# Cross-attention and linear attention on one core: interleaved last groups, four tile places, early sums, one ones-product per visit, maxima through DRAM

## The chip, the cores and the metric
One core of a Trainium2 chip runs the whole program. The metric is device time in microseconds (us) from start to end of one execution; the figure for a kernel is the median of its runs. Engines: TensorE (PE in the profile; its weight loads are PEld), VectorE (DVE), ScalarE (ACT), GpSimd (POOL) and SyncE (SP), whose queue issues all DMAs here. TensorE has a granted clock, given as a share of 2.4 GHz.

## The reference
Two layers on x (4 batches, 1024 rows, 512 features) and a context of the same size, all fp32.

```python
# layer 0: attention with 16 heads of 32, softmax, output projection, residual, layer norm
Q, K, V = x @ Wq.T + bq, ctx @ Wk.T + bk, ctx @ Wv.T + bv       # split in 16 heads
out = softmax(Q K^T / sqrt(32)) V @ Wo.T + bo
x = layernorm(out + x) * gamma0 + beta0
# layer 1: linear attention with phi = elu
KV = phi(ctx)^T ctx;  Z = 1 / (phi(x) . sum(phi(ctx)) + 1e-6)
x = layernorm(x + (phi(x) @ KV) * Z) * gamma1 + beta1
```

## The kernel before
**Units.** Heads go in groups of four (128 features); there are 16 groups (4 per batch). A unit is one group and one chunk of 256 queries: 64 units, of 16 ticks each, so 1024 ticks in which scores are computed. In tick k TensorE makes one 128x512 block of scores (`pass1`, L258), only for its row maxima (VectorE, L553). LEAD = 22 ticks later `pass2` (L282) makes the scores again the other way round (keys on partitions), with the row maximum subtracted inside the matmul: rows 96 to 103 of `q_stack` hold the negated maxima, those of `k_stack` a one-hot pattern. ScalarE takes the exponential into `p_ring` (L451, eight key tiles deep).

**Visits.** Every 8 ticks, from VISIT_AT = 35 on, TensorE visits four key tiles: `visit` multiplies the exponentials with V into `acc` (L300, 32 records) and sums them with a matrix of ones for the denominators (L308). For the sums GpSimd first adds the key tiles in pairs (`add_pair`, L760), in two halves of 512 columns. A visit takes two pair sums, 8 matmuls of 256 columns each, recorded as 16. `pair_sum` has two places, and a pair waits for the product of the pair two before it (`T["divided"]`). There are 128 visits. VectorE's `normalise` then inverts and scales `acc` into `outT` (20 units deep).

**Maxima.** VectorE's `split_max` reduces the maxima of a unit to `max_row` and splits them in two fp32r parts, `neg_max`. At tick 19 of the unit (PLACE) TensorE turns them with four matmuls (`place_max`, L267) in one of the score banks, and ScalarE copies the result into `q_stack` (L441).

**Chains.** The other work of TensorE is cut in chains, of which one piece is made in a tick (`beside`): K and V (projections of half a group's keys, 4 ticks), Q (a unit's queries, 2), O (output projection of one tile of 128 rows, 4), T (turning phi, 1), A (phi times KV, 4), S (one quarter of KV of a batch, 8 pieces), N (the sum of phi over the keys, 1), B (the bias of V through Wo, once, 4). A planner written in Python chooses the tick of each chain: no chain starts before `earliest`, the one with the first `deadline` goes first, and the table `after` holds what must be done before and how many ticks ago. All engines' queues are written out in the order of these ticks; SP's queue too, with waits in between. S needs `context_features`: two ScalarE operations and one on VectorE (L688) for each piece, and GpSimd's `add_features`.

**Tiles.** A tile of 128 rows goes O, y sum (L634), statistics, GpSimd's root (L773), ScalarE normalise (L473), GpSimd gamma and beta (L782, L784), ScalarE (L481, L483), phi (L656), T, A (L367), second norm, GpSimd gamma and beta (L789, L791), store. x, y and the feature arrays share the memory of the context (`ctx_nat`); there are two places (NX = 2), so tile i waits for the store of tile i - 2. A batch's tiles start when its last group is done, so those of the last batch run at the very end.

**The start.** FIRST = -44: K, V, Q chains of the first units stand before tick 0.

## Time and profile before

| what | value |
|---|---|
| runs | 1761.07, 1754.87, 1755.48 us; median 1755.48 |
| profiled execution | 1762.24 us, of which the span of the trace is 1760.9 |
| TensorE busy | 1646.2 us (93%), weight loads 1114.6 beside it |
| VectorE / ScalarE / GpSimd busy | 1070.9 / 880.9 / 951.3 us |
| granted clock, mean | 0.972 |
| DMA | 168 MB, mean 95 GB/s |

How to read it: a row of the stage view has a stretch (us from the span's start), its length, the busy time of PE, PEld, DVE, ACT and POOL with their numbers of instructions, the granted clock, the DMA engines' share and GB/s. A row by line has line, engine, operation, output<-input, shapes and count, then busy us, mean ns of one, and idle time just before them with what ended most of it. A row in order of time has start, duration, engine, line, operation, count, and in brackets the idle time before it. Durations of matmuls are modelled and overlap, so a stretch is better read from starts.

### The profile page before, as it was taken

How to read it: one execution, taken by the hardware profiler on the slowest of the kernel's cores; microseconds unless marked ns; L12 is line 12 of the kernel's file. 1: busy time of each engine (PE TensorE's matmuls, PEld its weight loads, DVE VectorE, ACT ScalarE, POOL GpSimd, SP SyncE). 2: the span in 40 equal slices, each digit the busy share in tenths (PEclk: the TensorE clock that was granted, in tenths of full speed). 3: DMA queues.
4: the chain of work that ended last, by engine and by line, in shares of the span. 5: the costliest groups of instructions: out<-in, count | busy, mean ns of one | idle time of the engine just before them, and what ended most of it. 6: DMA issues, size and time to landing. Idle time of an engine off the chain costs nothing.

```text
span 1760.9 us, 32310 instructions
## 1 busy us (share of the span) xinstructions
PE 1646.2 (93%) x12176; PEld 1114.6 (63%) x12176; DVE 1070.9 (61%) x2216; ACT 880.9 (50%) x1617; POOL 951.3 (54%) x923
## 2 busy tenths in 40 slices
PE   6999999999999999999999999999999999999754
PEld 4667776676766666567666657657676767665321
DVE  2665557656666666567566756666666666666232
ACT  0355547555554554654554554665545554575321
POOL 0244535455655664455665655555566555566644
PEclk8999999999999999999999999999999999999877
DMA  8524162233315244141523234322322423200001
GB/s 252 159 63 132 55 204 78 73 99 103 108 40 138 79 130 162 55 115 39 144 79 110 74 103 146 110 85 91 112 72 91 122 74 102 97 24 13 25 24 36
DMA packets 149291, 168.05 MB, mean 95 GB/s; under 512 B 12816, under 2 KB 111120, under 8 KB 149136
## 3 DMA queue, kind: packets, MB, share of 16 engines
q1 hardware_dynamic: 149136, 165.99, 31.8%
q8 instruction: 97, 1.59, 0.4%
q14 instruction: 58, 0.48, 0.1%
HBM read 124.00 MB, written 41.94 MB: 94 GB/s over the span
## 4 chain that ended last, share of the span: by engine, by line
PE 81%; DVE 6%; POOL 4%; DMA 4%; issue 3%; ACT 2%; SPq 1%; DVEq 0%; ACTq 0%; POOLq 0%
PE acc L300 13%; PE score L258 13%; PE scoreT L282 12%; PE misc L375 6%; PE misc L329 6%; PE misc L367 6%; PE acc L308 6%; PE misc L339 6%; PE misc L351 5%; PE misc L319 4%; DVE maxes L553 2%; POOL pair_sum L760 1%; PE score L267 1%; DMA res_out<-ctx_nat 1%; DMA ctx_nat<-ctx_in 1%
## 5 line engine op out<-in xcount | busy, mean ns | idle before, releaser
L760 POOL TENSOR_TENSOR pair_sum<-p_ring 128x512 f32<-128x512 f32 x512 | 654.5, 1299 | 636.0 <-PE acc L308 568.5
L553 DVE TENSOR_REDUCE maxes<-score 128x1 f32<-128x512 f32 x1024 | 679.1, 678 | 441.6 <-PE score L258 440.5
L451 ACT ACTIVATE p_ring<-scoreT 128x512 f32<-128x512 f32 x1024 | 595.6, 594 | 616.8 <-PE scoreT L282 603.5
L258 PE MATMUL score<-k_stack,q_stack 96*128 96x512 f32 x1024 | 615.6, 603 | 8.7 <-DVE maxes L553 7.5
L282 PEld LDWEIGHTS scoreT<-q_stack,k_stack 104*128 104x128 f32 x2048 | 378.7, 191 | 187.8 <-ACT p_ring L451 114.4
L282 PE MATMUL scoreT<-q_stack,k_stack 104*128 104x256 f32 x2048 | 428.0, 291 | 16.3 <-ACT p_ring L451 14.8
L258 PEld LDWEIGHTS score<-k_stack,q_stack 96*128 96x128 f32 x1024 | 194.3, 190 | 170.4 <-issue 139.2
L300 PE MATMUL acc<-p_ring,v_sb 128*32 128x256 f32 x4096 | 279.4, 392 | 0.0
L300 PEld LDWEIGHTS acc<-p_ring,v_sb 128*32 128x32 f32 x4096 | 155.5, 112 | 81.6 <-ACT p_ring L451 22.2
L308 PE MATMUL acc<-pair_sum,ones 128*32 128x256 f32 x2048 | 159.3, 383 | 7.7 <-POOL pair_sum L760 7.7
L319 PE MATMUL misc<-xT_sb,wq 128*128 128x256 f32 x512 | 134.3, 386 | 10.1 <-DVE k_low L615 5.8
L329 PE MATMUL misc<-ctxT_sb,wk 128*128 128x512 f32 x256 | 133.2, 606 | 7.7 <-DMA ctxT_sb<-ctxT_in 6.9
L367 PE MATMUL misc<-kv_sb,ctx_nat 128*128 128x512 f32 x256 | 135.3, 623 | 4.5 <-issue 2.3
L339 PE MATMUL misc<-wv,ctxT_sb 128*128 128x128 f32 x1024 | 134.1, 275 | 0.0
L375 PE MATMUL misc<-ctx_nat,fphi_sb 128*128 128x512 f32 x256 | 132.1, 597 | 0.0
L351 PE MATMUL misc<-wo,outT 128*128 128x512 f32 x256 | 129.5, 597 | 0.0
L339 PEld LDWEIGHTS misc<-wv,ctxT_sb 128*128 128x128 f32 x1024 | 125.8, 192 | 0.6 <-DVE k_low L615 0.3
L308 PEld LDWEIGHTS acc<-pair_sum,ones 128*32 128x32 f32 x2048 | 87.2, 112 | 46.5 <-POOL pair_sum L760 10.0
L319 PEld LDWEIGHTS misc<-xT_sb,wq 128*128 128x128 f32 x512 | 90.2, 193 | 18.9 <-DVE k_low L615 6.0
L773 POOL TENSOR_TENSOR rstd<-var_eps,minus_half 128x1 f32<-128x1 f32 x64 | 36.5, 571 | 92.8 <-DVE var_eps L648 92.6
L441 ACT ACTIVATE q_stack<-score 8x1024 fp32r<-8x1024 f32 x64 | 65.0, 1016 | 41.5 <-PE score L267 41.0
L688 DVE SCALAR_TENSOR_TENSOR fphi_sb<-f_sb,ctx_nat 128x128 f32<-128x128 f32 x128 | 70.1, 547 | 22.6 <-ACT f_sb L506 11.0
(66 smaller groups left out, 1221.8 us busy)
## 6 DMA issues: line engine op xcount, KB each, us to landing
xT_sb<-xT_in SPq DMA_DIRECT2D x64, 512.0 KB, 4.1
k_stack<-k_dram SPq DMA_DIRECT2D x96, 256.0 KB, 4.4
q_stack<-q_dram SPq DMA_DIRECT2D x192, 128.0 KB, 2.5
ctxT_sb<-ctxT_in SPq DMA_DIRECT2D x8, 1024.0 KB, 7.3
k_dram<-k_high SPq DMA_DIRECT2D x32, 256.0 KB, 2.0
k_dram<-k_low SPq DMA_DIRECT2D x32, 256.0 KB, 2.6
q_dram<-q_high SPq DMA_DIRECT2D x64, 128.0 KB, 1.7
q_dram<-q_low SPq DMA_DIRECT2D x64, 128.0 KB, 1.9
```

Of the source, the lines that this page charges most:

```text
L258: pe.matmul(score[use % 3][:], q_stack[0:SPLIT, unit % NQ, j, t * P:(t + 1) * P], k_stack[0:SPLIT, unit // NC % 2 * QUAD + j, h * HALF:(h ...
L282: mm = pe.matmul(scoreT[k % 2][:, (j % 2) * CH:(j % 2 + 1) * CH], k_stack[0:ROWS, unit // NC % 2 * QUAD + j, kt * P:(kt + 1) * P], q_stack ...
L300: mm = pe.matmul(acc[j * DK:(j + 1) * DK, 0:CH], v_sb[:, group % 2, kt, j * DK:(j + 1) * DK], p_ring[:, n % NP, j * CH:(j + 1) * CH], star ...
L308: mm = pe.matmul(acc[j * DK:(j + 1) * DK, CH:2 * CH], ones[:, 0:DK], pair_sum[:, pair % 2, j * CH:(j + 1) * CH], start=False, stop=part == ...
L319: mm = pe.matmul(bank_of("Q", unit)[:, 0:CH], wq[:, t, :], xT_sb[:, unit % 2, t, :], start=t == 0, stop=t == G - 1)
L329: mm = pe.matmul(bank_of("K", i)[:], wk[:, t, :], ctxT_sb[:, h, t, :], start=t == 0, stop=t == G - 1)
L339: mm = pe.matmul(bank_of("V", i)[:, t * P:(t + 1) * P], ctxT_sb[:, h, f, t * P:(t + 1) * P], wv[:, f, :], start=f == 0, stop=f == G - 1)
L367: mm = pe.matmul(bank_of("A", tile)[:], phiT_sb[:, d * P:(d + 1) * P], kv_sb[:, d, :], start=d == 0, stop=d == G - 1)
L375: pe.matmul(bank_of("S", i)[:], fphi_sb[:, piece % NPHI, :], ctx_nat[:, t, :], start=t == 0, stop=t == KT - 1).then_inc(T["kv_piece"], 1)
L451: act.activation(p_ring[:, n % NP, h * HALF:(h + 1) * HALF], scoreT[k % 2][:], ACT.Exp, scale=SCALE).then_inc(A["exped"], 1)
L553: dve.reduce_max(maxes[:, unit % 2, t, j, h:h + 1], score[bank_use[k] % 3][:], AX.X).then_inc(V["maxed"], 1)
L760: pool.tensor_tensor(pair_sum[:, pair % 2, cols], p_ring[:, (n - 1) % NP, cols], p_ring[:, n % NP, cols], ALU.add).then_inc(L["paired"], 1)
```

## The change
Five things at once.

1. **One ones-product per visit.** After the pair sums, GpSimd adds the two pair sums of a visit for columns 0 to 511 (`add_quad`, 128 times), VectorE those of columns 512 to 1023 (its own `add_quad`, two ticks before the visit), and the visit makes one product. The two places of `pair_sum` alternate so that the odd pair alone waits for a product and the even pair for the two quad sums.
2. **Maxima through DRAM.** `place_max` goes on both engines. `neg_max` is 128x32, VectorE turns it in blocks of 32 (`max_turned`), SP writes four blocks of 16 rows x 128 B to DRAM (`put_max`) and reads them back over the four heads into `q_stack` (`stack_max`). LEAD goes from 22 to 26, and VISIT_AT to LEAD + 13.
3. **The first linear sums come early.** S of batch 0 may start at tick 0 (before: 176), its context is loaded at tick -14, FIRST is -24, B moves to `outT` as its source, `wq` has two places.
4. **The last batch's last two head groups take turns**: their eight units are ordered (0,0) (0,1) (1,0) (0,2) (1,1) (0,3) (1,2) (1,3) as (group, chunk).
5. **Four places for the last batch's tiles**, for x and y each, in the memory of `ctxT_sb`, which is free by then; x is loaded when the last K and V projections are done.

```diff
-    LEAD = 22
-    PLACE = 19
-    VISIT_AT = 35
-    FIRST = -44
+    LEAD = 26
+    VISIT_AT = LEAD + 13
+    FIRST = -24
+    def place_of_pair(pair):
+        return (pair // 2 + pair % 2) % 2
+    order = [(b, b * G + g, chunk) for b in range(B) for g in range(G) for chunk in range(NC)]
+    order[-2 * NC:] = [(B - 1, GROUPS - 2 + g, chunk) for g, chunk in
+                       ((0, 0), (0, 1), (1, 0), (0, 2), (1, 1), (0, 3), (1, 2), (1, 3))]
+    def slot_of(tile):
+        return tile % NX if tile < TILES - KT else NX + tile % 4
+    def before(tile):
+        if tile < TILES - KT:
+            return tile - NX
+        return tile - 4 if tile >= TILES - KT + 4 else -1
...
             if kind == "N":
-                return UT * UB * i + 200
+                return UT * UB * i + 200 if i > 0 else FIRST
             if kind == "S":
-                return UT * UB * b + 176 + 8 * t
-            unit = UB * b + UB - NC + t // TPC
-            spaced = UT * UB * b + 242 + TILE_TICKS * t
-            return max(UT * unit + 50, spaced if b < B - 1 else 0)
+                return UT * UB * b + 176 + 8 * t if b > 0 else 0
+            spaced = UT * UB * b + LEAD + 220 + (TILE_TICKS if b < B - 2 else TILE_TICKS - 4) * t
+            return max(UT * unit_at[G * b + G - 1, t // TPC] + LEAD + 28, spaced if b < B - 1 else 0)
...
-                for s in range(VISIT // 2):
-                    pair = VISIT // 2 * v + s
-                    pe.wait_ge(L["paired"], 2 * (pair + 1))
-                    for j in range(QUAD):
+                pe.wait_ge(L["quad_low"], v + 1)
+                pe.wait_ge(V["quad_high"], v + 1)
+                for j in range(QUAD):
...
+            def add_quad(v):                                   # VectorE
+                first, second = (pair_sum[:, place_of_pair(2 * v + i), HALF:2 * HALF] for i in range(2))
+                dve.wait_ge(L["paired"], 4 * (v + 1))
+                dve.tensor_tensor(first, first, second, ALU.add).then_inc(V["quad_high"], 1)
...
+                elif h == 0 and pair >= 2:                     # GpSimd, add_pair
+                    pool.wait_ge(L["quad_low"], pair // 2)
+                    pool.wait_ge(V["quad_high"], pair // 2)
...
+            def add_quad(v):                                   # GpSimd
+                first, second = (pair_sum[:, place_of_pair(2 * v + i), 0:HALF] for i in range(2))
+                pool.wait_ge(L["paired"], 4 * v + 3)
+                pool.tensor_tensor(first, first, second, ALU.add).then_inc(L["quad_low"], 1)
...
+            def put_max(unit):
+                sp.wait_ge(V["max_turned"], unit + 1)
+                if unit >= 2:
+                    sp.wait_ge(M[f"max_in{unit % 2}"], landed(unit - 2, 2, 1))
+                for block in range(QUAD):
+                    sp.dma_start(max_dram[unit % 2, :, block * DK:(block + 1) * DK],
+                                 max_turned[block * DK:block * DK + 2 * QUAD * TPC, unit % 2, :]
+                                 ).then_inc(M[f"max_out{unit % 2}"], 16)
+            def stack_max(unit):
+                sp.wait_ge(M[f"max_out{unit % 2}"], landed(unit, 2, QUAD))
+                sp.dma_start(q_stack[SPLIT:ROWS, unit % NQ, :, :].bitcast(F32),
+                             max_dram[unit % 2].rearrange("(r t) n -> r (t n)", t=TPC).unsqueeze(1).to_broadcast(
+                                 [2 * QUAD, QUAD, CH])).then_inc(M[f"max_in{unit % 2}"], 16)
...
+                unit, i = divmod(k - UT - 4, UT)
+                if i == 0 and 0 <= unit < UNITS:
+                    put_max(unit)
+                if i == 2 and 0 <= unit < UNITS:
+                    stack_max(unit)
```

## Rows read from the trace of the kernel before

**Rows 1.** The page, busy time of each engine (us, share, instructions).

```profile
PE 1646.2 (93%) x12176; PEld 1114.6 (63%) x12176; DVE 1070.9 (61%) x2216; ACT 880.9 (50%) x1617; POOL 951.3 (54%) x923
```

**Rows 2.** Stages, cut at score 0, 64, 256, 1023 and the last ones-product.

```profile
42.30:116.20 73.90, 70.63 (x475) 50.22 (x473) 47.90 (x89) 29.78 (x51) 23.96 (x20) 0.95 0.41 119
116.20:394.40 278.20, 271.39 (x2189) 191.49 (x2187) 170.52 (x338) 151.26 (x294) 137.17 (x130) 0.99 0.36 106
394.40:1615.90 1221.50, 1193.05 (x9029) 812.88 (x9028) 797.63 (x1655) 655.10 (x1204) 711.97 (x685) 0.99 0.32 94
1615.90:1663.40 47.50, 36.58 (x284) 20.71 (x282) 15.07 (x38) 21.36 (x36) 32.63 (x31) 0.91 0.07 23
1663.40:1760.90 97.50, 49.21 (x110) 21.51 (x106) 31.08 (x89) 19.74 (x29) 44.29 (x50) 0.73 0.08 27
```

**Rows 3.** Groups by line, all of the span.

```profile
L553 DVE TENSOR_REDUCE maxes<-score 128x1 f32<-128x512 f32 x1024 | 679.1, 678 | 441.6 <-PE score L258 440.5
L760 POOL TENSOR_TENSOR pair_sum<-p_ring 128x512 f32<-128x512 f32 x512 | 654.5, 1299 | 636.0 <-PE acc L308 568.5 <-ACT p_ring L451 67.2 <-issue 0.3
L688 DVE SCALAR_TENSOR_TENSOR fphi_sb<-f_sb,ctx_nat 128x128 f32<-128x128 f32 x128 | 70.1, 547 | 22.6 <-ACT f_sb L506 11.0 <-PE misc L375 6.9 <-issue 3.8
L773 POOL TENSOR_TENSOR rstd<-var_eps,minus_half 128x1 f32<-128x1 f32 x64 | 36.5, 571 | 92.8 <-DVE var_eps L648 92.6
```

**Rows 4.** Order of time, PE, a visit without maxima and full ticks.

```profile
742.74 1.93 PE L300 MATMUL acc<-p_ring,v_sb 128*32 128x256 f32 x32
744.49 1.05 PE L308 MATMUL acc<-pair_sum,ones 128*32 128x256 f32 x16
745.47 0.50 PE L258 MATMUL score<-k_stack,q_stack 96*128 96x512 f32 x1
...
746.51 0.80 PE L258 MATMUL score<-k_stack,q_stack 96*128 96x512 f32 x1
...
747.84 0.79 PE L258 MATMUL score<-k_stack,q_stack 96*128 96x512 f32 x1
```

**Rows 5.** Order of time, PE, a visit with maxima.

```profile
756.31 0.28 PE L267 MATMUL score<-ident,neg_max 128*8 128x128 f32 x1
...
759.44 0.50 PE L258 MATMUL score<-k_stack,q_stack 96*128 96x512 f32 x1
```

**Rows 6.** Order of time, DVE and ACT, ticks without a chain.

```profile
123.68 4.87 DVE L553 TENSOR_REDUCE maxes<-score 128x1 f32<-128x512 f32 x8 [3.12 <-PE score L258]
...
125.17 3.47 ACT L451 ACTIVATE p_ring<-scoreT 128x512 f32<-128x512 f32 x6 [0.17 <-PE scoreT L282]
```

**Rows 7.** Who waited for whom (total us, times, longest).

```profile
PE score L267 <- DVE neg_max L573: 15.8, 20, 1.4
```

**Rows 8.** One line, L656: durations in ns, min/median/max.

```profile
L656 DVE SCALAR_TENSOR_TENSOR ctx_nat<-ctx_nat x32: 682/1124/1741, 393.0 to 1743.5; 128x512 f32<-128x512 f32 x32
```

**Rows 9.** DMA issues (KB each, median us to landing), and one issue in time.

```profile
q_stack<-q_dram SPq DMA_DIRECT2D x192, 128.0 KB, 2.5
...
q_dram<-q_low SPq DMA_DIRECT2D x64, 128.0 KB, 1.9
...
bq_col<-bq_in SPq DMA_DIRECT2D x1, 2.0 KB, 5.3
...
33.40 0.43 SPq L881 DMA_DIRECT2D q_dram<-q_low  x1
```

**Rows 10.** The first 50 us as a stage.

```profile
0.00:50.00 50.00, 31.91 (x117) 20.89 (x117) 15.21 (x21) 4.08 (x6) 1.25 (x11) 0.87 0.84 252
```

**Rows 11.** Order of time, the end.

```profile
1687.99 1.26 POOL L768 TENSOR_TENSOR ctx_nat<-ctx_nat,bo_row 128x512 f32<-128x512 f32 x1 [4.87 <-DMA ctx_nat<-x_in]
...
1699.58 0.69 DVE L634 TENSOR_TENSOR ctx_nat<-misc,ctx_nat 128x512 f32<-128x512 f32 x1 [8.36 <-POOL ctx_nat L768]
...
1708.65 0.69 DVE L656 SCALAR_TENSOR_TENSOR ctx_nat<-ctx_nat 128x512 f32<-128x512 f32 x1 [3.43 <-ACT ctx_nat L483]
...
1748.68 3.67 PE L367 MATMUL misc<-kv_sb,ctx_nat 128*128 128x512 f32 x8 [0.73 <-DVE ctx_nat L678]
```

More of the change, by code:

```diff
@@ L137, in landed, with landed_tile @@
         def landed(index, slots, each):
             return 16 * each * (index // slots + 1)
-        bank_use, bank_freed = {}, []
-        for k in range(HALVES + PLACE):
-            if k < HALVES:
-                bank_use[k] = len(bank_freed)
-                bank_freed.append((V["maxed"], k + 1))
-            if k % UT == PLACE % UT and k >= PLACE:
-                bank_use["max", (k - PLACE) // UT] = len(bank_freed)
-                bank_freed.append((A["max_placed"], (k - PLACE) // UT + 1))
+        def landed_tile(tile):
+            return landed(tile, NX, 1) if tile < TILES - KT else landed(tile - TILES + KT, 4, 1)
@@ L424, in tensor_program @@
                 beside(k)
-                unit, i = divmod(k - PLACE, UT)
-                if i == 0 and 0 <= unit < UNITS:
-                    place_max(unit)
                 v, i = divmod(k - VISIT_AT, 2 * VISIT)
@@ L434, in scalar_program @@
             act = nc.scalar
-            def place_max(unit):
-                use = bank_use["max", unit]
-                act.wait_ge(T["max_turned"], unit + 1)
-                if unit >= NQ:
-                    act.wait_ge(T["scoredT"], UT * (unit - NQ + 1))
-                act.activation(q_stack[SPLIT:ROWS, unit % NQ, :, :],
-                               score[use % 3][SPLIT:ROWS, 0:CH].unsqueeze(1).to_broadcast([2 * QUAD, QUAD, CH]),
-                               ACT.Copy).then_inc(A["max_placed"], 1)
             def exponential(k):
@@ L528, in scalar_program @@
                     keep_kv(number_of)
-                if i == 0 and 0 <= unit < UNITS:
-                    place_max(unit)
                 piece = sum_piece(k + 4)
@@ L594, in normalise @@
                     if unit >= NO:
[L595 removed]
+                        b, _, chunk = order[unit - NO]
                         dve.wait_ge(T["o_projected"], KT * b + TPC * (chunk + 1))
@@ L715, in vector_program @@
                 unit, i = divmod(k - UT, UT)
-                if 0 <= unit < UNITS and i < 3:
+                if 0 <= unit < UNITS and i < 4:
                     split_max(unit, i)
@@ L790, in affine1 @@
                 pool.wait_ge(L["scaled1"], tile + 1)
-                pool.tensor_tensor(x_nat[:, tile % NX, :], y, beta1_row[:], ALU.add).then_inc(L["result"], 1)
+                pool.tensor_tensor(x_nat[slot_of(tile)], y, beta1_row[:], ALU.add).then_inc(L["result"], 1)
             def add_features(piece):
@@ L842, in gpsimd_program @@
                     add_pair(pair, i)
+                if 0 <= pair < KT * UNITS // 2 and pair % 2 and i == 2:
+                    add_quad(pair // 2)
         def sync_program():
@@ L868, in load_xT @@
             def load_xT(unit):
-                b, _, chunk = unit_of(unit)
+                b, _, chunk = order[unit]
                 if unit >= 2:
@@ L982, in sync_program @@
             for s in range(NX):
-                sp.wait_ge(M[f"out{s}"], 16 * TILES // NX)
+                sp.wait_ge(M[f"out{s}"], 16 * (TILES - KT) // NX)
+            for s in range(NX, NX + 4):
+                sp.wait_ge(M[f"out{s}"], 16 * KT // 4)
         gpsimd_program()
```

240 lines of the change are left out of this document (126 added, 114 removed).

## Prediction

> **What bounds the kernel now.** I read the page's totals first, then the busy time by stage, then TensorE's order of time inside one unit, and the waits last. TensorE is busy 1646 of 1760.9 us; no other engine passes 1071 [rows 1]. The stages [rows 2] say the same of the two long middle stretches (271 of 278 us, 1193 of 1222), while the last 97.5 us are another matter: 49 us busy at a granted clock of 0.73. So a cut on TensorE counts in the middle, and a cut in latency at the end. Everything is ordered by the planner's ticks: a tick is one score matmul, one scoreT pair and, where a chain runs, one piece of a chain. With a chain piece a tick takes 1.33 us (scores at 746.51 and 747.84) [rows 4]; I call it a full tick. Without one, VectorE's maxima (8 in 4.87 us) and ScalarE's exponentials (6 in 3.47 us) set the pace, 0.60 us a tick [rows 6], and with the small delays around it I use 0.69: a light tick.
>
> **Part 1, one ones-product per visit.** From the first ones-product at 744.49 to the next score at 745.47 a visit spends 0.98 us on 16 records; the change keeps 8. 128 visits x 0.49 = 63 us on the engine that bounds.
>
> **Part 2, maxima off TensorE.** A visit with place_max lasts 3.13 us (756.31 to 759.44), one without 2.73 (742.74 to 745.47) [rows 4, 5]: 0.40 x 64 = 26 us. TensorE also sat 15.8 us waiting for neg_max at these matmuls [rows 7], in the light stretches where VectorE is just in time. Both go: 41 us. ScalarE loses 64 copies; its wait before exponentials is idle time anyway.
>
> **Part 3, what takes their place.** (a) GpSimd adds 128 half-width sums of the kind of L760, 1.30 us each [rows 3] = 166 us, to 951 busy. Nearly all its idle time before L760 was waiting for the ones-products (568.5 us) [rows 3]. The new buffer rule removes half of that wait: the even pair of a visit no longer waits for a product. (b) VectorE adds 128 sums with two SBUF inputs of 128x512. The trace has no such add; the nearest is L656, same size and two SBUF inputs: 682 ns at least, 1124 median, 1741 at most [rows 8]. The long ones overlap GpSimd. I take 1.1 us, 141 us in all, bounds 0.68 and 1.74 (87 and 223 us). (c) A 128x32 transpose per unit on VectorE, which no row has; between nothing and the 0.68 us of a 512-wide operation [rows 8], 44 us at most, and I take 0.2, 13 us. VectorE goes from 1071 to about 1230, GpSimd to 1117, of some 1640: neither is the bound by its sum. By order they can be: the VectorE add stands two ticks before its visit, waits for GpSimd's pair sum, and the maxima of the next ticks queue behind it; three score banks let TensorE run about two ticks ahead, and the visit (over 2 us without scores) lets VectorE catch up. From nothing to one GpSimd add (1.3 us) per visit may come through; I take 0.1 us, 13 us.
>
> The shared read path decides (b). The trace has L656 at 0.68 us alone and 1.74 at most [rows 8], about one GpSimd add more. The Trainium skill, SBUF — State Buffer, Who interferes with whom, says that a VectorE instruction with two SBUF inputs and a GpSimd one that reads SBUF shut each other out for the whole instruction. By that rule each add could cost 0.7 + 1.3 = 2.0 us when GpSimd's own quad sum has just begun, and 0.7 otherwise; it would put the 141 us between 87 and 250.
>
> (d) The maxima go by four writes of 2 KB and one read. Issue 0.43 us each, landing 1.9 us (q_dram) and 2.5 us (q_stack) [rows 9]: 4 x 0.43 + 1.9 + 0.5 + 2.5 = 6.7 us after the transpose at tick +3 of the next unit; the scoreT pass needs them at +10, and a visit lies between. Cover: 7 x 1.33 + 2.2 = 11.5 us in full stretches, 7 x 0.60 + 2.2 = 6.4 in light ones. So about nothing in full, 0.3 to 2 us in light units. These writes have rows of 128 B. The nearest DMA of 2 KB in small pieces, bq_col, took 5.3 us among the start's loads [rows 9]; with that the chain takes 10.1 us and light units pay 3.7. I take 12 us over all, bounds 0 and 75 (20 light or mixed units). The Trainium skill, DMA: Bandwidth & Descriptors, Anatomy of one DMA, gives a fixed cost of about 2.0 us per DMA; two of them would leave the light cover as thin as I have it. Behind SP's two waits stand put_queries, xT loads and stack_queries, each needed a unit later.
>
> **Part 4, the first linear sums come early.** The planner's rules, worked through, put the 4 S chains of batch 0 at ticks 0 to 38 instead of 176 to 211. Their 32 pieces leave stretch 64 to 256 (109 chain ticks become 76): 33 x 0.62 = 20 us saved. In ticks 0 to 25 no scoreT runs (LEAD is 26 now), and with S pieces VectorE has a maximum (0.68) and a feature (0.55) each tick [rows 3]: 1.25 us x 26 = 32 us. Ticks 26 to 63 are almost all full: 35 x 1.33 + 3 x 0.6 = 48, and four visits at 2.73 give 11. Together 92 us for ticks 0 to 63, where before takes 73.9 [rows 2]. The start itself: DMA engines are 84% busy in the first 50 us [rows 10], and the change adds a wq block and eight context loads (2 MB) issued before the second query block. Score 0 stays at about 43 us, but S piece 0 waits for the whole context: 8 x 0.43 us of issue and about 7 us of landing put it near 50. No row shows it; it is 0 if the loads overlap, 12 if they are queued behind all else.
>
> **Part 5, the end.** Last scores at 1615.9, last ones-product at 1663.4, then 97.5 us: three rounds of two tiles [rows 2, 11]. Each round waits for a place: the result must be stored, the next x read (GpSimd waits 4.87 us at 1687.99), then the tile's own chain, 9.8 us from y's sum to phi (1699.58 to 1709.34) [rows 11]. With four places and interleaved groups the planner ends at tick 1097 instead of 1133; after the last visit (tick 1055) only O of tiles 30 and 31, and T and A of tiles 28 to 31 are left. From the last score to the last visit: 14 ticks of 1.1 (a full tick without its score), 12 of 0.6, 4 visits of 2.3 = 32 us, with 8 of waiting for GpSimd, which has four visits there (5 sums of 1.3 each, 6.4) and two to three tiles (five operations of 1.26 [rows 11], two roots of 0.57 and two shifts [rows 3]: about 7.9 each). Then, from the last ones-product: 5 for the division of the last unit, which stands in VectorE's queue around phi of tile 28, and for T28; O30 and O31 at 3.5 each (8 records of 512 columns, as A has in 3.67 [rows 11]); A28 3.7; T and A of tiles 29, 30 and 31 at 5 each (3.7, and 1.3 for the turn and ScalarE's copy): 31; 3 more for stretches at the lower granted clock; and 8.5 from the last product (1748.68 + 3.67) to the end [rows 11]: 42 us. 32 + 8 + 42 = 82 where before has 145.0.
>
> **Sum by stage, against the profiled span** [rows 2]. Start 50 (42.3). Ticks 0 to 63: 92 (73.9). 64 to 255: 278.2 less 24 x 0.49, less 12 x 0.6 at place_max, less 20 = 239. 256 to 1023: 1221.5, less 96 x 0.49, less 48 places (30), plus 18 more chain ticks x 0.64 (12) = 1157. End 82. Total 1620. New waits 13 + 12 = 25. 1645 us of span; the profiled execution took 1762.24 with 1.3 outside, and the median is 6.8 below, so **1638 us** as a median, 7% faster.
>
> **Rivals.**
> A. The maxima come late. For: 128 B rows, SP's queue, light stretches. Against: 11.5 us of cover where most units are. Price 3.7 x 20 = 74 instead of 12: 1700.
> B. The end does not shrink as planned, because GpSimd saturates from tick 982 on: eight tiles x 7.9 + ten visits x 6.4 = 127 us of its work over a stretch in which TensorE wants 97. Then the 30 us come on top: 1668.
> C. Slower: VectorE's add, behind GpSimd's, delays the scores. If none of 1.3 + 0.7 us is absorbed, 128 x 2.0 = 256 us less the 13 taken: 1880. It decides from 0.9 us unabsorbed per visit on. Against: three banks, and VectorE's idle 2.4 to 3 us at each visit.
> D. New waits do not appear, and GpSimd's freer order removes some old ones: 1638 - 25 - 15 = 1598.
> E. The sums early don't pay: covered in the start, where 0 or 12 us move it within the range.
>
> **Chances.** Forecast (1615 to 1660) 0.52, A 0.15, B 0.16, C 0.05, D 0.12. A measurement of this kernel can tell about 0.5%, 9 us, from no change. Range 1592 to 1705: it leaves out C, half of D's lower side and A's worst. Faster by over 0.5%: 0.93, within: 0.02, slower: 0.05.
>
> **What would show it.** In the profile after: 1024 records of the ones-product instead of 2048; a plain visit of 2.2 to 2.3 us; full ticks still 1.33; from the last ones-product to the end about 42 us; GpSimd near 1117 busy, VectorE near 1230. Wrong for A: TensorE idle before scoreT, released by a DMA to q_stack. For C: full ticks longer than 1.4 near visits, TensorE waiting for L553. For B: TensorE waiting for pair_sum in the last 100 us. For part 4: TensorE idle after score 0, released by a feature.

## The result, and the profile after

The changed kernel took 1706.5 us as a median of four runs (1704.4 to 1713.9) where before took 1757.0, now a median of four runs too: a ratio of 0.972 [0.968, 0.975], 50 us less. The prediction said 1638, in a range of 1592 to 1705. The direction held, and less than half of the 119 us came. The profiled execution spans 1707.0 us, against the 1645 us of the prediction's sum.

The page's totals and groups of the kernel after (the last four rows from the groups by line with shapes kept apart; columns: busy us, mean ns of one | idle us before it, and its releasers):

```profile
span 1707.0 us, 30458 instructions
PE 1583.3 (93%) x10896; PEld 1040.8 (61%) x10896; DVE 1237.9 (73%) x2409; ACT 813.5 (48%) x1553; POOL 1138.1 (67%) x1051
L775 POOL TENSOR_TENSOR pair_sum<-p_ring 128x512 f32<-128x512 f32 x512 | 654.9, 1294 | 286.5 <-DVE pair_sum L582 161.1 <-ACT p_ring L448 121.8
L582 DVE TENSOR_TENSOR pair_sum<-pair_sum 128x512 f32<-128x512 f32 x128 | 131.8, 1030 | 19.5 <-POOL pair_sum L775 19.2
L318 PE MATMUL acc<-pair_sum,ones 128*32 128x256 f32 x1024 | 80.5, 387 | 8.3 <-DVE pair_sum L582 4.8 <-POOL pair_sum L782 3.3
L570 DVE TENSOR_TENSOR neg_max<-max_row,neg_max 128x8 fp32r<-128x8 f32 x64 | 35.7, 558 | 0.0
```

The engines' totals are those of the sum: VectorE 1238 (about 1230 foreseen), GpSimd 1138 (1117), 1024 records of the ones-product. VectorE's add costs 1.03 us (1.1 taken). By the rule of the Trainium skill cited in the prediction (SBUF — State Buffer, Who interferes with whom) it would lie between 0.7 and 2.0 us. For this line (L582) the trace gives 668 ns at least, 682 median and 1793 at most, so it agrees. GpSimd no longer waits for products. It waits for VectorE's half of the quad sum instead (161.1 us). TensorE's own waits for the two halves are short, 4.8 and 3.3 us in all.

A plain visit in TensorE's order of time, after, with two full ticks behind it:

```profile
746.74 1.94 PE L311 MATMUL acc<-p_ring,v_sb 128*32 128x256 f32 x32
748.49 0.61 PE L318 MATMUL acc<-pair_sum,ones 128*32 128x256 f32 x8
749.04 0.50 PE L279 MATMUL score<-k_stack,q_stack 96*128 96x512 f32 x1
750.07 0.80 PE L279 MATMUL score<-k_stack,q_stack 96*128 96x512 f32 x1
751.40 0.79 PE L279 MATMUL score<-k_stack,q_stack 96*128 96x512 f32 x1
```

746.74 to 749.04 is 2.30 us, against 2.73 [rows 4]. The saved product is worth 0.43 us, not 0.49. A full tick is 1.33 us (750.07 to 751.40), as before. So the pieces are almost what they were said to be; the loss lies between them. By stage, after, cut at the same scores and at the last one (columns as in [rows 2]):

```profile
43.84:142.10 98.26, 90.50 (x486) 57.39 (x486) 61.75 (x127) 45.80 (x113) 40.93 (x50) 0.94 0.39 117
142.10:394.60 252.50, 238.90 (x1884) 166.17 (x1880) 182.05 (x341) 119.43 (x211) 152.67 (x123) 0.97 0.37 109
394.60:1613.90 1219.30, 1164.65 (x8072) 766.13 (x8068) 939.37 (x1824) 609.51 (x1166) 867.58 (x797) 0.97 0.33 97
1613.90:1707.00 93.10, 65.24 (x361) 33.40 (x359) 45.95 (x108) 35.39 (x59) 75.69 (x72) 0.86 0.08 29
```

Tick 64 comes at 142.1, and the prediction said 50 + 92 = 142. Ticks 64 to 255 take 252.5 (239 foreseen, new waits aside), the end 93.1 (82). Most of the miss is in ticks 256 to 1023: 1219.3 where 1157 was foreseen and before took 1221.5, so the stage in which the change takes the most work off TensorE gained nothing. Two things show in its row beside [rows 2]. TensorE's idle time, span less busy, went from 28 to 55 us. And the granted clock went from 0.99 to 0.97, so that what TensorE still does takes longer.

What it waits for, the waits after (columns: us in total, times, longest):

```profile
PE score L279 <- DVE maxes L549: 24.0, 43, 1.3
PE scoreT L293 <- DMA q_stack<-max_dram: 20.2, 12, 5.6
PE score L279 <- DMA k_stack<-k_dram: 10.7, 2, 5.7
```

The second is the rival "the maxima come late", with 12 cases and 20.2 us. The longest of them in order of time, with the queue (SPq) that issues the transfers:

```profile
1369.76 2.09 SPq L921 DMA_DIRECT2D max_dram<-max_turned  x4
...
1374.79 0.35 SPq L967 DMA_DIRECT2D ctx_nat<-x_in  x1
1375.24 1.32 SPq L945 DMA_DIRECT2D k_stack<-k_dram  x3
1376.60 0.33 SPq L927 DMA_DIRECT2D q_stack<-max_dram  x1
...
1381.76 0.80 PE L293 MATMUL scoreT<-q_stack,k_stack 104*128 104x256 f32 x2 [5.63 <-DMA q_stack<-max_dram]
```

The read of the maxima is issued 4.7 us after the last of their writes. Before it in SyncE's queue stand the next x and three key loads (768 KB), and 2.5 of the 4.7 us (1372.31 to 1374.79) the queue stands still, since that x goes where a tile's result was, and waits for its store. The matmul that needs the maxima starts 5.2 us after the issue. The sum had counted 1.9 + 0.5 + 2.5 us from the writes on. This is the longest case. In ten of the twelve that can be followed through the trace, from the end of VectorE's transpose to the scoreT matmul it took 7.2 to 11.2 us, and 14.0 here, where the sum has 6.7. In nine of the ten the read itself was through in 1.9 to 3.9 us, so most of the excess lies ahead of its issue. Five of the ten fall in full stretches, where the prediction counted on about nothing. Around the longest case in slices of 3 us (same columns):

```profile
1378.00:1381.00 3.00, 0.00 (x0) 0.00 (x0) 0.00 (x0) 0.00 (x0) 3.00 (x3) 0.97 1.05 221
1381.00:1384.00 3.00, 2.24 (x5) 1.27 (x5) 0.00 (x0) 0.60 (x1) 2.88 (x3) 0.50 0.38 77
1384.00:1387.00 3.00, 3.00 (x7) 1.77 (x6) 0.69 (x1) 0.60 (x1) 0.00 (x0) 0.50 0.00 0
```

The 16 DMA engines are full (1.05) while the read is on its way. TensorE stands still for 5.63 us, and then the granted clock is 0.50, the lower of its two levels (1.2 GHz), for the next 6 us. So this wait costs its own length and then a stretch at half speed.

The first wait, for VectorE's maxima, has another source, at least where a unit starts. The start of a unit, after:

```profile
910.34 1.27 POOL L803 TENSOR_TENSOR ctx_nat<-ctx_nat,gamma_row 128x512 f32<-128x512 f32 x1 [1.51 <-ACT ctx_nat L470]
910.39 1.25 DVE L567 CAST neg_max<-max_row 128x8 fp32r<-128x8 f32 x1
...
911.70 1.27 POOL L805 TENSOR_TENSOR ctx_nat<-ctx_nat,beta_row 128x512 f32<-128x512 f32 x1
912.24 0.76 DVE L570 TENSOR_TENSOR neg_max<-max_row,neg_max 128x8 fp32r<-128x8 f32 x1
...
912.37 0.51 PE L279 MATMUL score<-k_stack,q_stack 96*128 96x512 f32 x1 [1.05 <-DVE maxes L549]
```

The cast and the subtraction of split_max have eight elements per partition, and take 0.15 us at their shortest. Here they take 1.25 and 0.76 us, and each ends when the GpSimd operation beside it ends (911.61 and 912.97). The subtraction's mean over the kernel is 558 ns, the cast's 498. All casts and subtractions of over 0.3 us (28 and 41 of 64) end within 0.1 us of a GpSimd operation. The division of the unit before (L589 to L604) is in the same ticks. The maxima queue behind all of it, and TensorE idles up to 1.3 us at a time.

### The profile page after: what moved, and what is told of

It is laid out like the page before. It is cut to its first block and busy times, and to the rows that moved or that the text cites. A ratio compares the mean times of both kernels' runs of the same rounds, so it can differ in the third digit from the quotient of the medians.

```text
span 1707.0 us, 30458 instructions
## 1 busy us (share of the span) xinstructions
PE 1583.3 (93%) x10896; PEld 1040.8 (61%) x10896; DVE 1237.9 (73%) x2409; ACT 813.5 (48%) x1553; POOL 1138.1 (67%) x1051
## 5 line engine op out<-in xcount | busy, mean ns | idle before, releaser
L775 POOL TENSOR_TENSOR pair_sum<-p_ring 128x512 f32<-128x512 f32 x512 | 654.9, 1294 | 286.5 <-DVE pair_sum L582 161.1
L279 PE MATMUL score<-k_stack,q_stack 96*128 96x512 f32 x1024 | 630.3, 616 | 37.8 <-DVE maxes L549 24.0
L293 PEld LDWEIGHTS scoreT<-q_stack,k_stack 104*128 104x128 f32 x2048 | 385.6, 195 | 211.9 <-ACT p_ring L448 114.2
L293 PE MATMUL scoreT<-q_stack,k_stack 104*128 104x256 f32 x2048 | 434.6, 295 | 36.0 <-DMA q_stack<-max_dram 20.2
L311 PE MATMUL acc<-p_ring,v_sb 128*32 128x256 f32 x4096 | 259.4, 396 | 0.0
L311 PEld LDWEIGHTS acc<-p_ring,v_sb 128*32 128x32 f32 x4096 | 123.7, 113 | 128.7 <-issue 36.7
L782 POOL TENSOR_TENSOR pair_sum<-pair_sum 128x512 f32<-128x512 f32 x128 | 170.4, 1331 | 0.0
L582 DVE TENSOR_TENSOR pair_sum<-pair_sum 128x512 f32<-128x512 f32 x128 | 131.8, 1030 | 19.5 <-POOL pair_sum L775 19.2
L794 POOL TENSOR_TENSOR rstd<-var_eps,minus_half 128x1 f32<-128x1 f32 x64 | 40.8, 637 | 95.2 <-DVE var_eps L655 95.2
L695 DVE SCALAR_TENSOR_TENSOR fphi_sb<-f_sb,ctx_nat 128x128 f32<-128x128 f32 x128 | 79.4, 620 | 23.2 <-ACT f_sb L505 15.8
L318 PE MATMUL acc<-pair_sum,ones 128*32 128x256 f32 x1024 | 80.5, 387 | 8.3 <-DVE pair_sum L582 4.8
```

Source lines behind the costliest of these rows:

```text
L279: pe.matmul(score[k % 3][:], q_stack[0:SPLIT, unit % NQ, j, t * P:(t + 1) * P], k_stack[0:SPLIT, group_of[unit] % 2 * QUAD + j, h * HALF:( ...
L293: mm = pe.matmul(scoreT[k % 2][:, (j % 2) * CH:(j % 2 + 1) * CH], k_stack[0:ROWS, group_of[unit] % 2 * QUAD + j, kt * P:(kt + 1) * P], q_s ...
L311: mm = pe.matmul(acc[j * DK:(j + 1) * DK, 0:CH], v_sb[:, group % 2, kt, j * DK:(j + 1) * DK], p_ring[:, n % NP, j * CH:(j + 1) * CH], star ...
L775: pool.tensor_tensor(pair_sum[:, place_of_pair(pair), cols], p_ring[:, (n - 1) % NP, cols], p_ring[:, n % NP, cols], ALU.add).then_inc(L[" ...
L782: pool.tensor_tensor(first, first, second, ALU.add).then_inc(L["quad_low"], 1)
```

## The experiments

The ratio is each kernel's time over before's on the same chip, with its 95% interval. Differences between kernels of different calls are taken between ratios, times 1757 us; the changed kernel's own interval is 6 us to either side, which all of those carry. The stage figures come from the profiled executions, cut as above.

**The two sums of a visit left out** (the even pair's sum alone goes into the product, so half of each denominator is left out):

```
-                pe.wait_ge(L["quad_low"], v + 1)
-                pe.wait_ge(V["quad_high"], v + 1)
+                pe.wait_ge(L["paired"], 4 * (v + 1))
...
-                if i == 0 and 0 <= v < VISITS:
-                    add_quad(v)
```

> The changed kernel without its two sums of a visit on VectorE and GpSimd; the one ones-product takes the first pair sum alone, so half of the denominators is left out. It says what the sums cost. Theory V (the 62 us missing between ticks 256 and 1023 come mostly from VectorE's queue: its sums, and maxima queued behind them): the ratio to the kernel before falls from 0.972 to about 0.945 (1660 us), and TensorE's idle time before scores (24 us, released by L549) nearly goes. Theory M (the maxima's way through DRAM costs most): at most 15 us gained, 1690.

Measured: 0.959 [0.956, 0.962], 1685.3 us. The sums cost 22 us, where the prediction put 13 us of new waits beside them. Seven of them are in the end (86.1 us instead of 93.1), where GpSimd is the bound.

**Both sums on GpSimd:**

```
-                dve.tensor_tensor(first, first, second, ALU.add).then_inc(V["quad_high"], 1)
+                if 0 <= pair < KT * UNITS // 2 and pair % 2 and i in (2, 3):
+                    add_quad(pair // 2, i - 2)
```

> The changed kernel with both halves of the visit's sum on GpSimd (128 more additions of 1.3 us there, 166 us; VectorE loses 132 us). Theory V: 10 to 25 us faster than the changed kernel, 1680 to 1695. Rival G (GpSimd is the late one in the tile stretches): slower, 1720 to 1750, with TensorE waiting for pair_sum.

Measured: 0.984 [0.980, 0.987], 21 us slower than the change; TensorE waits 33.1 us for GpSimd's sum. Sharing the sum between the engines is right.

**VectorE's sum two ticks later:**

```
-                v, i = divmod(k - VISIT_AT + 2, 2 * VISIT)
+                v, i = divmod(k - VISIT_AT, 2 * VISIT)
```

> The changed kernel with VectorE's sum two ticks later, behind the maximum of the visit's own tick, so that no maxima before the visit queue behind it; the visit's first products (1.7 us) cover it. Theory V: 10 to 20 us faster than the changed kernel, about 1690. If GpSimd's lateness decides: within 5 us, since the sum then ends later and the visit and the next even pair on GpSimd wait for it.

Measured: 0.986 [0.982, 0.991], 26 us slower: the visit then waits for the sum (TensorE 23.5 us for VectorE's half, 4.8 in the changed kernel). So the sum where it stands does not stop the scores by much. That, with the 22 us of all sums, is the end of rival C at its price of 243 us.

**The maxima's way left out** (put_max and stack_max are not issued, and the maxima's rows of q_stack are zero, so the exponentials are not shifted; split_max and its transpose remain):

```
-                    pe.wait_ge(M[f"max_in{unit % 2}"], landed(unit, 2, 1))
...
-                    put_max(unit)
...
-                    stack_max(unit)
```

> The changed kernel without the maxima's way through DRAM: 320 DMAs less, the rows of q_stack for the maxima are zero, so the exponentials are taken without the maximum subtracted; VectorE's work stays. Theory M: the waits for the maxima go (20 us idle on TensorE before scoreT), and what follows them: 30 to 45 us faster than the changed kernel, 1665 to 1675. Theory V: 20 us, 1687.

Measured: 0.955 [0.951, 0.958], 1676.5 us. The way through DRAM costs 30 us, not 12. The idle time shown above is 20.2 us; the rest is consistent with the lower clock behind it, since the lost clock, (1 - granted clock) summed over slices of 6 us of ticks 256 to 1023, is 18.7 us here and 30.6 in the changed kernel.

**Maxima by TensorE again** (part 2 undone: place_max, its ScalarE copy and the bank table are back, LEAD is 22 again, the rest of the change stays):

```
-    LEAD = 26
+    LEAD = 22
+    PLACE = 19
...
+                    place_max(unit)
```

> The changed kernel with part 2 undone: the maxima are turned on TensorE and copied by ScalarE again, LEAD = 22; the other four parts stay. By the prediction's sum part 2 gains 41 - 12 = 29 us, so this would be 1735. Theories C and M: what part 2 saves on TensorE it gives back in waits, so this is within 15 us of the changed kernel, 1692 to 1722.

Measured: 0.991 [0.989, 0.992], so part 2 with its LEAD of 26 is worth 33 us; the prediction has 41 less 12. But its waits say more than its time:

```profile
PE score L298 <- DVE neg_max L604: 67.9, 53, 3.6
```

In the kernel before TensorE waited 15.8 us for these numbers [rows 7]. Here it waits 67.9, and the subtraction has grown from 290 ns to 838. Something else of the change has made VectorE's split late.

**Part 1 alone, put into the kernel before** (place_of_pair, both add_quad, one product per visit, and nothing else):

```
+                if h == 0 and pair >= 2 and pair % 2:
+                    pool.wait_ge(T["divided"], pair // 2)
+                elif h == 0 and pair >= 2:
+                    pool.wait_ge(L["quad_low"], pair // 2)
+                    pool.wait_ge(V["quad_high"], pair // 2)
```

> The kernel before with part 1 alone. By the prediction's sum: 50 us faster, 1706. Theory L: place_max, which waits for the steps of neg_max on VectorE, now waits much longer than before (68 us in the kernel with part 2 undone, 16 before), so the gain is 5 to 25 us, 1732 to 1752.

Measured: 1.011 [1.010, 1.013], 1782.0 us: slower than before. The group in the kernel before, by shape:

```profile
L573 DVE TENSOR_TENSOR neg_max<-max_row,neg_max 128x8 fp32r<-128x8 f32 x64 | 18.6, 290 | 0.0
```

The same group and the wait with part 1 alone:

```profile
L575 DVE TENSOR_TENSOR neg_max<-max_row,neg_max 128x8 fp32r<-128x8 f32 x64 | 52.6, 822 | 0.0
PE score L271 <- DVE neg_max L575: 66.7, 53, 2.7
```

VectorE and GpSimd around one split_max of this kernel, in order of time:

```profile
139.00 0.16 DVE L572 CAST neg_max<-max_row 128x8 fp32r<-128x8 f32 x1
139.06 0.68 DVE L583 TENSOR_TENSOR pair_sum<-pair_sum 128x512 f32<-128x512 f32 x1
...
139.91 2.50 POOL L774 TENSOR_TENSOR pair_sum<-p_ring 128x512 f32<-128x512 f32 x2 [2.48 <-DVE pair_sum L583]
140.27 0.94 DVE L575 TENSOR_TENSOR neg_max<-max_row,neg_max 128x8 fp32r<-128x8 f32 x1
```

This is part 1's hidden price, and it has two pieces. With VISIT_AT = 35, VectorE's own add_quad falls on tick 1 of a unit, so in 63 of 64 units it stands between the cast (tick 1) and the subtraction (tick 2), 0.76 us on average. And it is what GpSimd's next pair sum waits for, which in 45 of the 63 units starts before the subtraction ends: 59 of 64 subtractions take over 0.3 us and end with a GpSimd operation, where it was 13 before. From the start of the cast to the end of the subtraction takes 2.64 us on average, 1.41 before, so the maxima are ready some 1.2 us later in each unit, and TensorE's wait goes from 15.8 to 66.7 us. Roughly worked out: 51 us of new wait, less 128 x 0.43 = 55 for the products, plus 22 for the sums is +18 us; measured +20. That it comes so close is partly luck, since the 22 are from the changed kernel, and the lost clock, 15 us more here than before in ticks 256 to 1023, is left out. The prediction placed VectorE's add by its visit, two ticks ahead, and never asked what stands behind it in VectorE's queue at that tick. No run moves the add alone, so how much of the 51 us is the add and how much the longer subtraction is open.

**Part 1 undone in the changed kernel** (two products per visit, no quad sums):

```
-                for j in range(QUAD):
+                for s in range(VISIT // 2):
+                    pair = VISIT // 2 * v + s
+                    pe.wait_ge(L["paired"], 2 * (pair + 1))
+                    for j in range(QUAD):
```

> The changed kernel with part 1 undone: two ones-products per visit, no sums of sums, GpSimd's pairs wait for the products as before. By the prediction's sum part 1 gains 63 less 13: this would be about 1756. Leaving out only the sums gained 22 us, so TensorE's own saving minus that gives 1735 to 1745. Theory L (part 1 also makes GpSimd busy where VectorE's small two-input steps run, and these then wait): 1710 to 1730, and the steps of neg_max are back near 0.3 us.

Measured: 0.987 [0.985, 0.989]. Part 1 is worth 26 us once the maxima are off TensorE, 33 by the medians, against 50 foreseen and a loss of 20 alone. The two parts depend on each other: with LEAD = 26 VectorE's add falls on ticks 5 and 13, away from the split. The expectation that the split's steps would be near 0.3 us again without part 1 failed: cast and subtraction take 586 and 492 ns here, 498 and 558 with part 1, and TensorE waits 23.8 us for the maxima in place of 24.0. So nothing of the hidden price is seen in the changed kernel, and 55 less 22 = 33 us is all that part 1 had to give.

**Linear sums late again** (part 4 undone for batch 0):

```
-                return UT * UB * b + 176 + 8 * t if b > 0 else 0
+                return UT * UB * b + 176 + 8 * t
```

> The changed kernel with the first linear sums at tick 176 again (FIRST, wq and the rest stay). The prediction has part 3 cost 6 us net (26 at the start against 20 between ticks 64 and 256): 1700. Rival: the early sums fill ticks that are otherwise set by VectorE and ScalarE, so that undoing them loses 5 to 15 us: 1712 to 1722.

Measured: 0.965 [0.963, 0.968], 12 us faster than the change by the ratios and 6 by the medians. The prediction's own terms for part 4 (8 for the start, 18 for ticks 0 to 63, less 20) add up to a loss of 6. Its stages here: 81.0 us for ticks 0 to 63 and 274.1 for 64 to 255, beside 98.3 and 252.5.

**The old end** (last groups one after the other, two places for the tiles):

```
-    order[-2 * NC:] = [(B - 1, GROUPS - 2 + g, chunk) for g, chunk in
-                       ((0, 0), (0, 1), (1, 0), (0, 2), (1, 1), (0, 3), (1, 2), (1, 3))]
...
-        return tile % NX if tile < TILES - KT else NX + tile % 4
+        return tile % NX
```

> The changed kernel with the last batch's units in plain order and two places for its tiles, as before the change. The prediction gives the end 50 to 60 us: about 1760. Rival: part of what the end gains is lost between ticks 832 and 960, where the second-to-last group's keys are needed two units earlier (5.7 us of waiting for k_stack) and tiles stand closer: 1745 or less.

Measured: 0.995 [0.992, 0.997]. The new end is worth 41 us. In the profiled executions it saves 60 us behind the last score (153.3 to 93.1) and costs 20 us ahead of it (1199.1 against 1219.3 for ticks 256 to 1023). Part of the 20 is seen as a wait, in the changed kernel:

```profile
1472.29 0.77 PE L279 MATMUL score<-k_stack,q_stack 96*128 96x512 f32 x1 [5.66 <-DMA k_stack<-k_dram]
```

With turns (0,0), (0,1), (1,0) the last group's keys are wanted two units earlier.

**The division two ticks later**, on ticks 2 to 5 of a unit in place of 0 to 3, so half of it away from split_max:

```
-                unit, i = divmod(k - (VISIT_AT + 2 * VISIT + 1), UT)
+                unit, i = divmod(k - (VISIT_AT + 2 * VISIT + 3), UT)
```

> The changed kernel with the four steps of normalise (the division of a unit) two ticks later on VectorE. With LEAD = 26 they fall on ticks 0 to 3 of a unit, where the four steps of split_max are too; before they fell on ticks 12 to 15. Theory C (this collision delays the maxima of these ticks and the way of the maxima to DRAM): 10 to 20 us faster than the changed kernel, 1687 to 1697. Rival: the sum of VectorE's work counts, not its order: within 5 us; or the first visit of the next unit, at tick 7, now waits for the division: slower by up to 10.

Measured: 1.001 [0.998, 1.003], 51 us slower. A new wait takes over. TensorE's first product of the next visit needs acc, which the division still reads:

```profile
PE acc L311 <- issue: 41.1, 33, 3.5
```

The profile names no releaser here; by the program the wait before a unit's first visit is for the division's last step, and in the trace that step now stands behind VectorE's add of tick 5 (905.33, 905.92, and TensorE from 906.43). So this kernel could not say whether division and split disturb each other. The next two move everything together.

**LEAD 28 and LEAD 30:** two or four more ticks between a unit's scores and its scoreT pass, which also moves visits and division by as much:

```
-    LEAD = 26
+    LEAD = 28
```

> The changed kernel with LEAD = 28, between 26 (1706) and 30 (1696): visits fall on ticks 9 and 1, the division on ticks 2 to 5, half of it still beside split_max; the queries have five ticks. If the collision decides: near 1706 or in between. If the maxima's way decides (two more ticks suffice): 1690 to 1698.

> The changed kernel with LEAD = 30 (visits, divisions and exponentials four ticks later): the division falls on ticks 4 to 7, the maxima have 11 ticks for their way instead of 7. Theories C and M together: 20 to 40 us faster than the changed kernel, 1670 to 1685. Rival Q: the three places of q_stack are now free only three ticks before the next unit's scores, so those wait for the query blocks, 64 x 1 us or more: no gain or slower, 1700 to 1740, with TensorE idle before scores released by a DMA to q_stack.

Measured: LEAD 28 0.944 [0.943, 0.946], 1663.9 us; LEAD 30 0.965 [0.963, 0.967], 1696.2 us. At 28 the kernel is 48 us faster than the change by the ratios and 43 by the medians, more than the 30 us of the maxima's way. Its expectation had nothing below 1690. Stages of LEAD 28:

```profile
41.40:134.30 92.90, 86.48 (x441) 55.38 (x442) 61.11 (x125) 44.07 (x110) 37.85 (x48) 0.94 0.41 123
134.30:371.70 237.40, 232.09 (x1883) 163.74 (x1881) 168.02 (x342) 118.13 (x211) 150.87 (x122) 1.00 0.40 116
371.70:1570.60 1198.90, 1157.86 (x8106) 763.79 (x8105) 925.13 (x1827) 611.13 (x1170) 868.45 (x797) 0.98 0.33 98
```

Ticks 64 to 255 are the clearest: the same work (1883 and 1884 matmul records), 237.4 us instead of 252.5, and the foreseen number was 239. 6.8 of the 15.1 us are busy time, at a clock of 1.00 instead of 0.97, and 8.3 are idle time. The same light stretch in slices of 2 us, first in the changed kernel, then at LEAD 28:

```profile
312.00:314.00 2.00, 0.91 (x4) 0.67 (x5) 2.00 (x6) 1.19 (x2) 2.00 (x2) 1.00 0.49 173
314.00:316.00 2.00, 1.72 (x14) 1.09 (x18) 2.00 (x5) 0.97 (x2) 0.04 (x1) 0.96 0.03 3
316.00:318.00 2.00, 2.00 (x24) 1.07 (x20) 1.18 (x2) 0.22 (x1) 1.85 (x2) 0.50 0.06 17
```

```profile
296.00:298.00 2.00, 2.00 (x11) 1.47 (x10) 2.00 (x7) 1.80 (x4) 2.00 (x2) 1.00 0.11 35
298.00:300.00 2.00, 1.63 (x12) 1.06 (x14) 2.00 (x5) 1.30 (x3) 1.56 (x2) 1.00 0.03 3
```

VectorE is full in the slices of both (2.00); division and split are near each other in both. In the changed kernel TensorE falls to 0.91 busy of 2 us, and the visit that follows meets the lower level. In order of time, changed kernel:

```profile
313.83 0.50 PE L279 MATMUL score<-k_stack,q_stack 96*128 96x512 f32 x1 [0.76 <-DVE maxes L549]
...
315.52 3.38 PE L311 MATMUL acc<-p_ring,v_sb 128*32 128x256 f32 x32
```

3.38 us instead of 1.94 for the same 32 records. VectorE at LEAD 28, in the slices before those shown:

```profile
295.49 0.16 DVE L570 TENSOR_TENSOR neg_max<-max_row,neg_max 128x8 fp32r<-128x8 f32 x1
295.57 0.45 DVE L589 STREAM_TRANSPOSE den_rows<-acc 128x256 f32<-128x256 f32 x1
```

The split's subtraction takes its 0.16 us and is over as the division begins, TensorE stays busy, and the clock holds. The subtraction's mean over the kernel is 310 ns (558 at LEAD 26), and TensorE's waits at LEAD 28 are:

```profile
PE score L279 <- DVE maxes L549: 12.1, 37, 1.2
PEld scoreT L293 <- DMA q_stack<-max_dram: 1.0, 2, 0.7
PE score L279 <- DMA k_stack<-k_dram: 13.8, 2, 8.6
```

The wait for the maxima's way is gone, the one for VectorE halved, and the one for the last group's keys is longer. The short subtraction alone is not what makes LEAD 28 good: at LEAD 30 VectorE's add is on tick 1 again and the subtraction's mean is 795 ns, yet TensorE waits only 7.6 us for the maxima there. At LEAD 30 another appears, since q_stack has three places and a query block stays in use longer:

```profile
PE score L279 <- DMA q_stack<-q_dram: 17.7, 29, 1.5
```

**LEAD 28 without the maxima's way** (left out as above):

```
-    LEAD = 26
+    LEAD = 28
...
-                    put_max(unit)
...
-                    stack_max(unit)
```

> LEAD = 28, and the maxima's way through DRAM left out (the exponentials are taken without the maximum subtracted). Two ticks more of LEAD gave 43 us; leaving out the way at LEAD = 26 gave 30. If the way is covered at 28: within 6 us of 1664, and the other 13 us come from where visits and division fall on VectorE. If a part of the way is still paid at 28: 1640 to 1655.

Measured: 0.942 [0.939, 0.946]. Against 0.944 for LEAD 28 with it, the way costs nothing that can be measured. The same removal at LEAD 26 gave 0.955, so 21 us (0.955 to 0.942; 17 by the medians) of what LEAD 28 brings have nothing to do with the maxima's way; they come from where all that LEAD moves (exponentials, pair sums, visits, division) falls in the unit. By stage the two are well apart: without the way, LEAD 28 takes 238.3 us for ticks 64 to 255 where LEAD 26 takes 250.8, and 1191.3 for ticks 256 to 1023 where LEAD 26 takes 1190.3. In the long stage nothing but the way is gained.

**LEAD 28 with two products per visit:**

```
-    LEAD = 26
+    LEAD = 28
...
+                for s in range(VISIT // 2):
```

> LEAD = 28 with part 1 undone. It says what one ones-product per visit is worth when the phase of the ticks does not hide it. The prediction's sum: 50 us, so 1714. At LEAD = 26 it was 33. If the sums of sums cost more than the 13 us of the prediction also here: 30 to 40 us, 1694 to 1704.

Measured: 0.981 [0.978, 0.984]. Here part 1 is worth 64 us, more than the 50 net of the forecast and even than the 55 of the products, and much more than the 26 at LEAD 26. The subtraction's mean is 951 ns without part 1 and 310 with it, although GpSimd waits for the products here as before: its length follows the position of the engines' work, and not GpSimd's freedom. What makes up the 64 was not taken apart.

**LEAD 28 and the last group's turns one unit later:**

```
-                       ((0, 0), (0, 1), (1, 0), (0, 2), (1, 1), (0, 3), (1, 2), (1, 3))]
+                       ((0, 0), (0, 1), (0, 2), (1, 0), (0, 3), (1, 1), (1, 2), (1, 3))]
```

> LEAD = 28, and the last two head groups take turns one unit later, (0,0) (0,1) (0,2) (1,0) (0,3) (1,1) (1,2) (1,3). At LEAD = 28 TensorE waits 8.6 us once for the last group's keys, which can only be loaded when the third-to-last group is through. With a unit more that wait goes; the first tiles of the last batch start a unit later. If the wait is on the path: 5 to 9 us faster than 1664. If the end takes it back: within 3 us.

Measured: 0.942 [0.939, 0.945], 1659.2 us, the best of all; its interval meets that of LEAD 28 alone. Ticks 256 to 1023 take 1175.7 us instead of 1198.9, the end 108.5 instead of 95.1: more than half of what is won in the middle is given back behind it.

**The same with the linear sums late:**

```
-                return UT * UB * b + 176 + 8 * t if b > 0 else 0
+                return UT * UB * b + 176 + 8 * t
```

> LEAD = 28, turns one unit later, and the first linear sums at tick 176 again. The early sums cost 6 us at LEAD = 26. If the three add up: 1650 to 1655, ratio 0.938. If the early sums gain once the visits no longer collide: 1658 to 1666.

Measured: 0.945 [0.942, 0.948]. At LEAD 28 the place of the linear sums makes no difference that can be told.

## Why the prediction was right in direction and too low

**Held.** The bound (TensorE in the middle, latency at the end); the engines' totals; the start and ticks 0 to 63, 142 us in both, with the first S piece at 51.0 us after 6.4 of idle time (near 50 foreseen); part 4's small loss; VectorE's add (1.03 us). Of the end, 44 us behind the last ones-product (42 foreseen), and 49 before it (40 foreseen), where GpSimd is the bound (45.5 us busy):

```profile
1660.02 1.26 POOL L782 TENSOR_TENSOR pair_sum<-pair_sum 128x512 f32<-128x512 f32 x1
1660.10 1.73 DVE L582 TENSOR_TENSOR pair_sum<-pair_sum 128x512 f32<-128x512 f32 x1 [3.04 <-POOL pair_sum L775]
...
1661.98 1.08 PE L318 MATMUL acc<-pair_sum,ones 128*32 128x256 f32 x8 [3.78 <-DVE pair_sum L582]
```

This is rival B's mechanism at a third of its price: TensorE waits 3.78 us for the last visit's sums, which GpSimd begins late and whose other half VectorE finishes only after GpSimd's (1661.83 and 1661.28).

**Held by luck: part 2's worth**, 33 us for 29 net. The kernel that measures it lost 67.9 us at place_max and not 15.8, so 52 us more went with part 2 than the sum has, and the way cost 18 more; about 30 us stay unaccounted for.

**Failed: part 3 (d), "I take 12 us over all".** The way costs 30. The step priced every DMA by its own issue and landing and noted that others stand behind it in SP's queue; it did not ask which stand ahead of it. From the transpose on the way takes 7.2 to 14.0 us in the late units where 6.7 were counted, and in full stretches too; in the longest case the read goes behind a store's landing, x and 768 KB of keys. This is rival A, lateness at TensorE: of the causes it names SP's queue is the one that the trace shows, at less than half of the rival's price. The 2.0 us per DMA that the prediction takes from the Trainium skill (DMA: Bandwidth & Descriptors, Anatomy of one DMA) stand there for DMAs that GpSimd issues. SyncE issues these, and the median landing of the four writes was 1.6 us, so the landings were not what was mis-sized.

**Failed: part 3's claim that only the sums and the maxima's way bring new waits (13 + 12 us).** LEAD had no term at all: 26 instead of 22 moves visits and division inside a unit, onto the ticks of the split. The prediction took LEAD as cover for the way and never as a shift of the order. LEAD 28 without the way is 21 us better than LEAD 26 without it, and the profiled executions put this in ticks 64 to 255 (12.5 us). The same step missed what VectorE's add stands in front of. With part 1 alone that costs 51 us of wait, where TensorE waits for the split directly. In the changed kernel it costs nothing that can be seen, which is the luck of LEAD = 26: the add had moved off the split's ticks.

**Failed: the sum's assumption that TensorE's work keeps its length.** Idle moments often brought the lower clock level behind them. Over ticks 256 to 1023 the lost clock is 8.5 us before, 30.6 after (27.3 at LEAD 28, 17.0 there with later turns). It does not follow the idle time in proportion: with the old end 52.7 us of idle time go with 22.2 of lost clock, with two products 49.2 with 15.4. Only the end had been given such a term (3 us).

**Sizes.** 0.43 us per product for 0.49: 8 us. Sums 22 for 13: 9 us. The new end's 20 us ahead of the last score, which part 5 costed at nothing. The end itself 93 for 82: 11, of which 7 are already in the sums. Together with 18 for the way and 21 for the places in the unit that makes some 80 us of the 62 missed: these overlap, since one idle moment can have two causes, and they cannot be added exactly. The long stage, 62 us above its 1157, is where most of it lies, and the removals show it there: 29 us shorter without the way (1190.3), 20 with the old end (1199.1), 13 without the sums (1206.2), and 6 for the products' size. Two slips are in the sum itself and are small: the four visits of ticks 0 to 63 are taken at 2.73 us and not at the 2.24 of part 1, and 1645 + 1.3 - 6.8 is 1639.5.

**From the other side.** At LEAD 28, where the cover suffices and the order is better, the profiled execution spans 1665.7 us, 21 above the forecast sum of 1645. It is another kernel than the forecast one, so this shows only that the sum was within reach. Score 0 to tick 64 is 92.9 (92), ticks 64 to 255 237.4 (239). The 1198.9 of the long stage (1157 and part of the 25 us of waits) is nearly met by later turns: 1175.7, though the end then takes 108.5 and not 82.

**Open.** How the 21 us divide between the division that shares ticks with the split and the places of the visits; the one kernel that moved the division alone ran into acc. Whether part 1 alone gives its 33 us when VectorE's add is kept off the ticks of the split. Whether a second acc bank, or split instructions with a single operand in the shared memory, would give more was not tried. What sets the length of the stretch at the lower clock was not looked at.

## What to carry to other kernels

An instruction added to an engine with a fixed order delays what stands behind it, and what it releases on another engine runs at that moment too: before booking the addition as covered, list the short instructions right behind it, above all those in front of the bounding engine. A number that means "ticks of lead" in a software pipeline is also a position of everything defined relative to it, so try its neighbours: here two ticks brought nearly as much as the whole change (43 to 48 us beside 50). A transfer's latency includes what stands ahead of it in its queue, waits for other transfers among it, and what fills the DMA engines when it runs, and an idle moment on TensorE has to be priced with the slow stretch that may follow it.

## What the chip showed that was not expected

- A cast and a subtraction of 128x8 elements on VectorE, 0.15 us at their shortest, took up to 1.27 and 1.22 us and ended together with the GpSimd operation beside them. Means of the subtraction: 290 ns before, 822 with part 1 alone, 558 in the changed kernel, 310 at LEAD 28, 951 there with two products.
- After 0.9 us of work in a slice of 2 us, TensorE's granted clock was 0.50 from 316 to 318, and a visit of 1.94 us took 3.38. After a stop of 5.63 us it stayed at 0.50 for 6 us.
- A 32 KB read behind 768 KB of other loads in one queue took about 5 us from issue to use, with the DMA engines at 1.05 of full; in most of the other late units it took 1.9.
